# Tower's first layer in parts behind layer 1 of later units, and a gather between GpSimd's products

## What is computed

```python
e = jnp.stack([tbl_0[ids[:, 0]], ..., tbl_31[ids[:, 31]]], axis=1)
for W in (W0, W1, W2):
    xk = jax.nn.relu(jnp.einsum('bmd,bhd,mhk->bkd', x0, xk, W))
    outs.append(jnp.sum(xk, axis=2))
z = jnp.concatenate(outs, axis=1)
h = jnp.concatenate([z, dense_ctx], axis=1)
h = jnp.maximum(h @ W_top1 + b_top1, 0.0)
h = jnp.maximum(h @ W_top2 + b_top2, 0.0)
y = h @ W_top3
```

## Time and profile before

| | |
|---|---|
| median of 3 runs | 629.24 us (629.12 to 630.5) |
| profiled execution | 628.08 us |
| its span | 626.2 us |
| mean granted clock of TensorE | 0.986 |
| busy: PE, DVE, ACT, POOL | 573.1, 547.3, 467.3, 457.8 us |
| matmuls of the tower, first to last | 589.46 to 623.7 us |

### The profile page before, as it was taken

How to read it: one execution, slowest core, us unless ns; L and a number is a source line. 1 busy time by engine, 2 the same in 40 slices (tenths; PEclk the granted TensorE clock), 3 DMA queues, 4 the chain that set the end, 5 groups by cost and what they waited for, 6 DMA issues and landing times.

```text
span 626.2 us, 9918 instructions
## 1 busy us (share of the span) xinstructions
PE 573.1 (92%) x2620; PEld 193.7 (31%) x2620; DVE 547.3 (87%) x298; ACT 467.3 (75%) x3337; POOL 457.8 (73%) x353
## 2 busy tenths in 40 slices
PE   0389879999999998999999999999998999999998
PEld 0144322323232333333232323323343333233332
DVE  0389997999999999999999999999998999999500
ACT  0146677979797969689797969696978959796521
POOL 6777887889896988888888979798788866174000
PEclk9999889999999998999999999999898999999999
DMA  4878795939495776949394949587593939363100
GB/s 98 248 224 303 288 408 183 416 123 412 149 392 205 300 280 235 363 161 415 118 416 127 411 173 360 222 310 288 198 397 102 416 124 421 134 270 66 28 0 0
DMA packets 39187, 153.17 MB, mean 245 GB/s; under 512 B 8493, under 2 KB 18585, under 8 KB 23771
## 3 DMA queue, kind: packets, MB, share of 16 engines
q1 hardware_dynamic: 23956, 144.33, 58.7%
q0 software_dynamic: 8192, 2.11, 3.3%
q10 hardware_dynamic: 6983, 6.11, 3.0%
HBM read 147.60 MB, written 4.92 MB: 244 GB/s over the span
## 4 chain that ended last, share of the span: by engine, by line
POOL 31%; PE 25%; issue 16%; DVE 13%; ACT 3%; DMA 2%; POOLq 0%; SPq 0%; DVEq 0%
PE acc L638 20%; POOL rows L398 18%; POOL prod_pool L411 12%; DVE prod L448 12%; PE x L729 2%; ACT x L504 2%; PE x L698 1%; DMA spread<-x_scratch 1%; ACT relu_out L516 1%; DMA rows<-table,ids_sb 1%; PE x L720 1%; PE x L706 1%; PE acc L698 0%; ACT x_pool L504 0%; PE acc L706 0%
## 5 line engine op out<-in xcount | busy, mean ns | idle before, releaser
L448 DVE TENSOR_TENSOR prod<-spread,x 128x2048 f32<-128x2048 f32 (+2 forms) x277 | 536.7, 2006 | 17.3 <-DMA spread<-x_scratch_half 7.1
L638 PE MATMUL acc<-prod,w 128*64 128x512 f32 (+1 forms) x2076 | 460.2, 580 | 49.5 <-DVE prod L448 38.6
L398 POOL DMA_INDIRECT rows<-table,ids_sb x256 | 242.7, 948 | 81.2 <-issue 76.8
L638 PEld LDWEIGHTS acc<-prod,w 128*64 128x64 f32 x2076 | 151.2, 140 | 341.7 <-issue 251.9
L411 POOL TENSOR_TENSOR prod_pool<-spread,x_pool 128x1024 f32<-128x1024 f32 (+1 forms) x93 | 214.9, 2346 | 40.6 <-ACT x_pool L504 40.1
L516 ACT ACTIVATE relu_out<-acc 128x16 f32<-128x16 f32 x960 | 161.1, 359 | 8.2 <-DVE xt L437 5.4
L516 ACT ACTIVATION_READ_ACCUMULATOR relu_out<-acc 128x1 f32 x960 | 161.6, 385 | 0.0
L504 ACT ACTIVATE x<-acc 64x512 f32<-64x512 f32 (+1 forms) x136 | 74.1, 545 | 89.4 <-PE acc L638 87.7
L523 ACT ACTIVATE relu_out<-relu_out 128x16 f32<-128x16 f32 x544 | 110.4, 388 | 0.0
L523 ACT ACTIVATION_READ_ACCUMULATOR relu_out<-relu_out 128x1 f32 x544 | 110.1, 374 | 0.0
L638 PE MATMUL acc<-prod_pool,w 128*64 128x512 f32 (+1 forms) x372 | 94.7, 586 | 0.3 <-POOL prod_pool L411 0.3
(11 more groups left out here) (25 smaller groups left out, 33.6 us busy)
## 6 DMA issues: line engine op xcount, KB each, us to landing
spread<-x_scratch SPq DMA_DIRECT2D x120, 1024.0 KB, 8.8
first<-x_scratch SPq DMA_DIRECT2D x15, 512.0 KB, 7.7
spread<-x_scratch_half SPq DMA_DIRECT2D x14, 512.0 KB, 7.1
rows<-table,ids_sb POOLq DMA_INDIRECT x256
x_scratch<-xt ACTq DMA_DIRECT2D x15, 256.0 KB
w<-w ACTq DMA_DIRECT2D x2, 512.0 KB, 4.8
spread<-x_scratch_half SPq DMA_DIRECT2D x4, 256.0 KB, 4.6
spread<-wt SPq DMA_DIRECT2D x2, 384.0 KB, 4.5
```

The lines of the kernel that those rows point to most:

```text
L398: nc.gpsimd.indirect_dma_start(rows[u % 2][:, j * D:(j + 1) * D], None, table, bass.IndirectOffsetOnAxis(ap=index, axis=0)).then_inc(gathe ...
L448: nc.vector.tensor_tensor(prod[:, at:at + count, 0:n], tiles(u, t, count), x[:, 0:n].rearrange("p (a n) -> p a n", a=1).to_broadcast([P, c ...
L638: last = nc.tensor.matmul(parts(to[K * blk:K * blk + K, 0:n]), w, side(moving[:, 0:2 * n], blk), start=start, stop=stop)
```

## The change

- The first layer's columns are cut into four batches of 128 (BATCH). For the first three, which hold units 0 to 12, the layer is computed early: a part is one group t of 128 outputs for one batch and both halves. EARLY_PARTS places one part in each of the units 5 to 13 and 15 and two in unit 14, on PE behind layer 1 of unit u+1, into x0's PSUM; ACT takes it out (bias and relu, into h_1) behind after_1(u+1).
- Behind the last unit PE does the second layer for half 0 on the first 384 columns, then the first layer for the last batch (into x2's PSUM, h_1_last), then the second layer for half 1 on the 384 columns and for both halves on the last 128, then the third layer for both halves.
- w_top1 has a place of its own, and the dense weights and inputs lie in partitions 64 and up of square; SP loads them in unit 2. Only w_top2 is loaded late.
- POOL issues one gather behind each of the first two products of each layer, in place of gathers that stood in runs behind them.
- To make room: RING 10 for 12, POOL_SLOTS 3 for 4, two relu_out for three (buffer_free adds ACT's waits), w_1b in a slot of prod_pool. ACT waits for the biases before its first store.

```diff
-RING = 12
+RING = 10
-POOL_SLOTS = 4
-EARLY = 4
-AHEAD = 7
+POOL_SLOTS = 3
+GATHERS_3 = 4
+GATHERS_2 = 7
+BETWEEN = 2
...
+BATCH = COLS // 4
+EARLY_PARTS = {5: (0, (0,)), 6: (0, (1,)), 7: (0, (2,)), 8: (0, (3,)), 9: (1, (0,)), 10: (1, (1,)), 11: (1, (2,)),
+               12: (1, (3,)), 13: (2, (0,)), 14: (2, (1, 2)), 15: (2, (3,))}
+SOON = 3 * BATCH
+def early_before(u):
+    return sum(len(EARLY_PARTS[v][1]) for v in EARLY_PARTS if v < u)
+def batch_units(batch):
+    return sum(1 for u in range(UNITS) if z_at(u) < (batch + 1) * BATCH)
...
-        square = sb("square", [M, N])
+        square = sb("square", [P, N])
-        relu_out = [sb(f"relu_out{i}", [P, BLK]) for i in range(3)]
+        relu_out = [sb(f"relu_out{i}", [P, BLK]) for i in range(2)]
+        relu_out.append(relu_out[0])
-        w_1b = sb("w_1b", [P, G, K])
+        w_1b = prod_pool[:, 0, 0:G * K].rearrange("p (t k) -> p t k", k=K)
+        w_top1 = sb("w_top1", [P, 3, H1])
+        h_1 = sb("h_1", [P, H1 // P, 2, SOON])
+        w_dense = [square[64 + M * g:64 + M * g + D, 0:H1] for g in range(2)]
+        dense = [square[64 + M * g:64 + M * g + D, H1:H1 + COLS] for g in range(2)]
...
+        def to_h1(i, g):
+            return x0[:, g * BLK + i * BATCH:g * BLK + (i + 1) * BATCH]
+        def to_h1_last(t, g):
+            return x2[:, g * BLK + t * BATCH:g * BLK + (t + 1) * BATCH]
         def to_y(g):
-            return x2[M * g:M * g + 1, g * BLK:(g + 1) * BLK]
+            return acc[g][M * g:M * g + 1, :]
...
             # SP, in the loop over u
+                if u == HALVES:
+                    for g in range(2):
+                        sp.dma_start(w_top1[64 * g:64 * g + K, :, :], wt1[0:3 * K, :].rearrange("(l k) n -> k l n", k=K)).then_inc(tower_in, 16)
+                        sp.dma_start(w_dense[g], wt1[3 * K:3 * K + D, :]).then_inc(tower_in, 16)
+                        sp.dma_start(dense[g], dense_t[g]).then_inc(tower_in, 16)
...
-            def products(u, layer):
+            def products(u, layer, ahead, first=0):
...
                     nc.gpsimd.tensor_tensor(prod_pool[:, k % POOL_SLOTS, 0:width(u)], tiles(u, t, 1)[:, 0, :],
                                             x[:, 0:width(u)], ALU.mult).then_inc(pool_ready, 1)
+                    if i < BETWEEN:
+                        gather(ahead, slice(first + i, first + i + 1))
+                for i in range(len(pool_tiles(layer, u)), BETWEEN):
+                    gather(ahead, slice(first + i, first + i + 1))
...
             for u in range(LAST - 1):
-                products(u, 2)
-                gather(u + 2, slice(AHEAD, None))
-                gather(u + 3, slice(0, EARLY))
-                products(u, 3)
-                gather(u + 3, slice(EARLY, AHEAD))
+                products(u, 2, u + 2, GATHERS_2)
+                gather(u + 2, slice(GATHERS_2 + BETWEEN, None))
+                gather(u + 3, slice(0, GATHERS_3))
+                products(u, 3, u + 3, GATHERS_3)
+                gather(u + 3, slice(GATHERS_3 + BETWEEN, GATHERS_2))
...
             # ACT
+            def buffer_free(u, layer):
+                if layer == 0 and u > 1:
+                    act.wait_ge(summed[2], u - 1)
+                if layer == 2:
+                    act.wait_ge(summed[0], min(u + 2, UNITS))
...
+            def early_h1(u):
+                batch, parts_of = EARLY_PARTS.get(u, (0, ()))
+                if parts_of:
+                    act.wait_ge(h1_soon_mm, early_before(u) + len(parts_of))
+                for i, t in enumerate(parts_of):
+                    for g in range(2):
+                        last = nc.scalar.activation(h_1[:, t, g, batch * BATCH:(batch + 1) * BATCH], to_h1(i, g), ACT.Relu,
+                                                    bias=b_1[:, t:t + 1])
+                    last.then_inc(h1_soon_out, 1)
...
+            act.wait_ge(small_in, 48)
             act.wait_ge(turned, 1)
             store_wrapped(act, 0)
...
                 after_1(u + 1)
+                early_h1(u)
                 sum_2(u)
...
+            for g in range(2):
+                act.wait_ge(h1_mm, 2 * (H1 // P - 1) + g + 1)
+                for t in range(H1 // P):
+                    nc.scalar.activation(h_1_last[:, t, g, :], to_h1_last(t, g), ACT.Relu, bias=b_1[:, t:t + 1]).then_inc(h1_out, 1)
...
             # PE
+            def sums_in(to, t, l, columns):
+                for g in range(2):
+                    own = slice(64 * g, 64 * g + K)
+                    last = nc.tensor.matmul(to(g), w_top1[own, l, t * P:(t + 1) * P], z[own, l, columns],
+                                            start=l == 0, stop=l == 2)
+                return last
+            def early_h1(u):
+                batch, parts_of = EARLY_PARTS.get(u, (0, ()))
+                columns = slice(batch * BATCH, (batch + 1) * BATCH)
+                if parts_of:
+                    pe.wait_ge(tower_in, 96)
+                if early_before(u):
+                    pe.wait_ge(h1_soon_out, early_before(u))
+                for i, t in enumerate(parts_of):
+                    for l in range(2):
+                        pe.wait_ge(summed[l], batch_units(batch))
+                        sums_in(lambda g: to_h1(i, g), t, l, columns)
+                    dense_in(lambda g: to_h1(i, g), t, columns)
+                    pe.wait_ge(summed[2], batch_units(batch))
+                    sums_in(lambda g: to_h1(i, g), t, 2, columns).then_inc(h1_soon_mm, 1)
...
                 layer(u, 2, order_of(2, u))
                 layer_1(u + 1)
+                early_h1(u)
                 if u + 1 < LAST:
                     layer(u, 3, order_of(3, u))
...
+            pe.wait_ge(h1_soon_out, 3 * (H1 // P))
+            pe.wait_ge(w_top2_in, 16)
+            for t in range(H2 // P):
+                to_layer_2(0, t, soon, h_1, False)
             for t in range(H1 // P):
                 for l in range(2):
                     pe.wait_ge(summed[l], UNITS)
-                    sums_in(t, l)
-                dense_in(t)
+                    sums_in(lambda g: to_h1_last(t, g), t, l, late)
+                dense_in(lambda g: to_h1_last(t, g), t, late)
                 pe.wait_ge(summed[2], UNITS)
...
+            for t in range(H2 // P):
+                to_layer_2(1, t, soon, h_1, False)
+            for g in range(2):
+                for t in range(H2 // P):
+                    to_layer_2(g, t, late, h_1_last, True)
+            pe.wait_ge(small_in, 48)
+            for s in range(H2 // P):
+                for g in range(2):
                     pe.wait_ge(h2_out, 2 * g + s + 1)
                     last = nc.tensor.matmul(to_y(g), w_top3[:, s:s + 1], h_2[:, s, g, :],
                                             start=s == 0, stop=s == H2 // P - 1)
+                    if s == H2 // P - 1:
+                        last.then_inc(y_mm, 1)
```

More of the change, by code:

```diff
@@ L373, in _ @@
                     load_first(2)
-            sp.wait_ge(prod_ready, made(3, LAST - 1))
[L376 to L382, removed]
+                if u == HALVES:
[3 more added lines that the diff above has]
+                        sp.dma_start(dense[g], dense_t[g]).then_inc(tower_in, 16)
+            sp.wait_ge(prod_ready, made(3, LAST - 1))
+            sp.dma_start(w_top2[:, :, :], wt2.rearrange("(s p) n -> p s n", p=P)).then_inc(w_top2_in, 16)
             for g in range(2):
@@ L540, in squares @@
                     act.wait_ge(square_free, u)
-                nc.scalar.activation(square[:, 0:width(u)], tiles(u, 0, 1)[0:M, 0, :],
+                nc.scalar.activation(square[0:M, 0:width(u)], tiles(u, 0, 1)[0:M, 0, :],
                                      ACT.Square).then_inc(square_ready, 1)
@@ L679, in layer, with dense_in @@
                 return done
+            def sums_in(to, t, l, columns):
[4 more added lines that the diff above has]
+                return last
+            def dense_in(to, t, columns):
+                for g in range(2):
+                    nc.tensor.matmul(to(g), w_dense[g][:, t * P:(t + 1) * P], dense[g][:, columns], start=False, stop=False)
+            def early_h1(u):
[3 more added lines that the diff above has]
+                    pe.wait_ge(tower_in, 96)
+                if early_before(u):
+                    pe.wait_ge(h1_soon_out, early_before(u))
[6 more added lines that the diff above has]
+                    sums_in(lambda g: to_h1(i, g), t, 2, columns).then_inc(h1_soon_mm, 1)
             pe.wait_ge(consts_in, 48)
@@ L693, in _, with to_layer_2 @@
             layer(LAST, 3, order_of(3, LAST))
-            def sums_in(t, l):
-                for g in range(2):
-                    own = slice(64 * g, 64 * g + K)
-                    last = nc.tensor.matmul(to_h1(t, g), w_top1[own, l, t * P:(t + 1) * P], z[own, l, :],
-                                            start=l == 0, stop=l == 2)
-                    if l == 2:
-                        last.then_inc(h1_mm, 1)
-            def dense_in(t):
```

(36 more changed lines are left out.)

46 lines of the change are left out of this document (17 added, 29 removed).

## The result

The changed kernel takes **619.99 us** (median of 4 runs, 617.91 to 621.07) where the kernel before took 629.18 beside it: a ratio of 0.9845, 95% interval 0.9813 to 0.9878. Its profiled execution took 619.01 (span 617.1, mean granted clock 0.992), against 628.08 before. The forecast was 618.0 and its sum for the profiled execution 616.9, so the end came 2.1 later than the sum. One of the twelve runs of the kernel in experiment 5 took 2094.1 us; it stands in that kernel's median but not in its ratio.

A forecast was written before the change was run, and what follows sets the result against it. POOL was taken to pace the loop, 0.3 us a unit over DVE, and PE alone the end; -13.2 + 1.0 + 0.5 + 1.6 - 1.1 = -11.2 took 629.24 to 618.0 us, 8-in-10 range 614.8 to 626.0.

The forecast's parts named there:

- The end: Behind the last product: first two tower layers 19.2 us for 32.4, -13.2; third layer and copies of y +1.0.
- Short pairs: TensorE pairs of 128 columns take 0.107 us, bounds 0.107 and 0.216; the rival that they don't shrink so had 14%.
- The parts in the loop: Units 5 to 13: a part takes 1.48 us, TensorE 33.6 a unit, 0.2 under POOL's pace; +0.5 together.
- Unit 14's second part: Unit 14's two parts make PE's layer 3 1.9 us later, 0.3 won back, passed on through ACT's x2: +1.6.
- POOL: Four gathers a unit moved between products save 0.1 us a unit, 33.8, over the eleven units POOL paces: -1.1.
- The lone gather: On POOL, a gather between products: 2.5 us from product to gather, 1.0 from gather to product, like a run's last.
- SP's loads come later behind the third product: SP's four loads wait for POOL's third product, 384.1 instead of 381.78; 2.9 us of slack, so no cost.
- Part 4: Remaining changes: smaller ring and slots, six tower loads in unit 2 (some 3.7 us of SP's queue), ACT's waits; loads cost nothing, at worst 1.
- rival 2: Loads or gathers land too late and DVE waits in layer 2: 0.6 us a unit, 13 times, 626; chance 10%.

The follow-up runs named there:

- experiment 5: Kernel before with only the ring cut from 12 to 10 and GpSimd slots from 4 to 3: 629.21 us beside 629.0.
- experiment 3: Changed kernel with early parts' matmuls issued twice, 629.57 us, or two of eight kept, 617.82; with tower loads first, four of eight issued again, 618.50.
- experiment 2: Changed kernel with the six tower loads issued right behind the ids, ahead of the first turn, instead of in unit 2: 616.65 us, 617.38 in another set.
- experiment 6: Changed kernel with tower loads right behind the ids, and GpSimd's old gather order: 619.96 us against 617.38 with the interleaved order.
- experiment 1: Two separate edits to the changed kernel: GpSimd's old gather order, 620.62 us; the six tower loads in unit 4 instead of unit 2, 620.07 us.

## Why the prediction was right, and where it was off

- **The end** (-13.2, then +1.0): measured 12.7 less, then 0.6 more, so 12.1 for 12.2. The halves of the third layer run side by side (1.88 for both, 1.7 taken, 3.4 the other bound). Each stretch of the other layers is 0.25 to 0.35 over its term: 5.35 for 5.1, 10.63 for 10.3 (0.33 a matmul for 0.32), 3.66 for 3.4 (0.114 for 0.107); the 0.4 that was counted apart for changes of shape lies in them.
- **Short pairs**: 0.107 to 0.112, at the lower bound, where the price was taken (in experiment 3 the second eight pairs add 1.28, of which 0.42 is the change of shape, so 0.107 each; four pairs add 0.45). The Trainium skill, TensorE: Matmul & The Clock Gate, section "Wait — 56ns, not 53.3ns?", has about 62 ns a matmul without hardware decode; the eight matmuls in 0.45 above are 56 ns each, so the estimate of 0.124 a pair that was worked out from it was not met here. No run here shows which way of decoding was on.
- **The parts in the loop** (+0.5; "33.6 a unit"): TensorE's need was right (33.54), and from the turn of unit 5 to that of unit 16 no such cost appears. What the prediction had in its own numbers (33.6 for TensorE, 33.58 for VectorE) but did not draw from them is that the two bind at the same length, measured to some 0.02.
- **Unit 14's second part** (+1.6): 0.8 by the stretch; VectorE's wait rose by 1.5 (1.89 for 0.37). The mechanism as given, through ACT's x2, is not the whole of it: with the part moved, that wait shrinks to 0.62 and the time stays. The bound in this stretch is TensorE's work, and the short waits that it and VectorE still met here before are gone.
- **POOL** (-1.1): GpSimd's unit, first product to first product, is 33.76 in the mean of three (242.85 to 344.12) for 33.87 before (273.07 to 374.68), so the 0.1 a unit came. But VectorE's turns are not 33.8 apart throughout: in units without a wait they come down to 33.56 (134.56 to 168.12 in experiment 2) and 33.57 (376.75 to 410.32 with the old order in experiment 6). So GpSimd does not set the length of every unit, and what it costs is read from VectorE's waits for rows. These fell by 1.0 and 1.7 in two pairs of kernels, the stretch that holds them by 0.1 and 1.8 (experiment 6). Over the whole stretch from the turn of unit 5 to that of unit 16, parts and order together gave 1.6 for 0.6; a part of that may lie in TensorE's granted clock, 1.00 from 205 to 509 for 0.98 before, where the gap of the earlier trace rows is filled now. No run separates it: with the parts and the old order the stretch took 375.25 in experiment 1 and 376.45 in experiment 6, for 376.72 before. The lone gather costs what was taken: a product starts 1.0 after it, a gather 2.54 after a product. That SP's loads come later behind the third product cost nothing that the scatter lets one see, as forecast (experiment 1).
- **The step that failed** is Part 4's line on the six tower loads, "nothing, at worst 1": they cost 2.7 at one turn. I counted their time on SP's queue and the slack of the loads behind them, but not the transfers themselves: some 4.9 us of all 16 engines at a place where these are full (252 GB/s instead of 357), and gathers in the same engines. It is rival 2's mechanism, once instead of thirteen times, and by another cause.
- **Not explained**: 1.1 up to the turn of unit 3. From the turn at 47.5 to that turn the kernel before takes 20.63, with ring and slots cut 20.19, the changed kernel and its ten variants 20.92 to 23.20. SP's first load of unit 2 waits there for a store (issued at 48.67, the load at 56.74; before 48.71 and 55.07). Neither the order of the gathers nor the place of the tower loads takes it out of that range, and the cut of ring and slots alone does not bring it about; which part of the change does remains open.

The two misses, +2.7 and +1.1, and two errors of -1.0 and -0.8 in the other pieces make the 2.0 by which the loop is later than forecast. That the pieces partly cancelled, and the total came out so near, was luck; that the end came out at 12.1 for 12.2 was not.

## What to carry to other kernels

Work moved from the end into a loop is free only up to the room of the engine that takes it; measure that room by issuing the moved work twice, since the busy share (96.9, then 99.6%) does not tell at what length the engine begins to set the pace. Loads that move along with it need a place where the DMA engines are idle, not merely where the issuing queue has time: here they held up the gathers in the same engines by 2.6 to 2.7 us. Reckon them by what their packets take, not by their bytes. And a wait that grows on one engine need not be the path: if moving its cause leaves the time as it was, look for the engine without gaps.

## What the runs showed of the hardware

- Six loads of 0.9 MB in all (two of 384 KB, four of 32 KB) drew the rate of full DMA engines down to 252 GB/s for 5 us (their 2 KB packets took 0.175 us each, the 8 KB packets around them 0.35), and cost 2.6 to 2.7 us of waiting at one turn in either of two units, but 0.6 to 1.0 ahead of the first turn.
- GpSimd's two stops between gathers came again where they had been, ahead of the 114th and the 226th of its 256 gathers in all thirteen kernels: in the changed kernel 1.98 ahead of the gather at 205.65 and 1.87 ahead of that at 444.19, elsewhere 1.8 to 3.1, and once 5.2 (the first stop with the tower loads in unit 4). The first is followed by VectorE's wait at 239.30. What stops GpSimd there, no run shows.
